# A two-layer GNN block on one core: layer 1's bias and first own part are loaded before layer 0's last transpose, the bounds are computed directly behind their input, and the first z load goes ahead of more of the count loads

## The reference

```python
# block 1: two GraphSAGE layers (mean over the edges, rows = src, cols = dst)
vals  = 1 / deg[rows]                                    # deg: edges per row, 0 -> 1
layer = lambda x, W, b: relu(concat([x, segment_sum(vals * x[cols], rows)]) @ W.T + b)
x = layernorm(x + layer(layer(x, W0, b0), W1, b1))
# block 2: the 32 largest of each row are sent along the edges
h_self, h_neigh = x @ W_self, x @ W_neigh
neigh = segment_sum(top32(h_neigh)[src], dst) / max(deg_dst, 1)
out = layernorm(x + h_self + neigh)
```

## Time and profile before

| | us |
|---|---|
| median of 3 runs | 649.02 (648.73 to 651.68) |
| the profiled execution's own time | 648.15 |
| its span | 646.4 |
| PE busy | 624.2 (97%) |
| DVE, ACT, POOL busy | 487.8, 314.6, 111.9 |
| DMA | 79.62 MB, mean 123 GB/s |
| mean granted TensorE clock | 0.989 |

### The profile page before, as it was taken

One profiled execution on the slowest core, in us unless ns is written; L12 is line 12 of the kernel. 1 busy time (PEld: TensorE's weight loads), 2 busy tenths in 40 slices (PEclk: granted clock), 3 DMA queues, 4 the chain that ended last, 5 costly groups with the idle time before them and its releaser, 6 DMA issues.

```text
span 646.4 us, 10800 instructions
## 1 busy us (share of the span) xinstructions
PE 624.2 (97%) x3750; PEld 322.9 (50%) x3751; DVE 487.8 (75%) x1273; ACT 314.6 (49%) x607; POOL 111.9 (17%) x188
## 2 busy tenths in 40 slices
PE   8689999999999999999998999999999999999996
PEld 4466677776444444444443444444444444444442
DVE  7988999998689998888835688888888910548533
ACT  5769999999397777766721222222232200001000
POOL 2232132222201110110102232232332200000000
PEclk9899999999999999999999999999999999999998
DMA  8535656655422332322214656556564399833200
GB/s 224 135 122 156 217 177 194 192 175 175 125 45 57 71 68 54 68 55 51 71 47 118 147 131 138 131 126 152 133 138 118 83 243 215 211 113 118 86 25 25
DMA packets 66742, 79.62 MB, mean 123 GB/s; under 512 B 30320, under 2 KB 59407, under 8 KB 66681
## 3 DMA queue, kind: packets, MB, share of 16 engines
q1 hardware_dynamic: 66681, 78.86, 47.0%
HBM read 38.91 MB, written 33.38 MB: 112 GB/s over the span
## 4 chain that ended last, share of the span: by engine, by line
PE 65%; ACT 14%; DVE 9%; DMA 7%; issue 3%; SPq 1%; ACTq 0%; POOL 0%; DVEq 0%; POOLq 0%
PE pair L1606 36%; PE bank L1702 8%; ACT slab L1128 7%; PE pair L1702 7%; PE bank L1507 5%; PE pair L1507 4%; DMA a<-z_dram 4%; PE bank L1533 2%; ACT ct L1167 2%; ACT a L1288 2%; DVE hots L673 2%; PE bank L1499 2%; ACT own L1185 1%; PE pair L1419 1%; DMA own_in<-own_dram 1%
## 5 line engine op out<-in xcount | busy, mean ns | idle before, releaser
L1606 PE MATMUL pair<-a,ct 125*128 125x512 f16 x625 | 140.0, 381 | 0.0
L1606 PE MATMUL pair<-xs,ct 125*128 125x512 f16 x625 | 139.1, 379 | 0.0
L1606 PEld LDWEIGHTS pair<-a,ct 125*128 125x128 f16 x625 | 62.5, 100 | 74.9 <-issue 2.1
L673 DVE TENSOR_TENSOR hots<-iota,jobs 125x1792 f16<-125x1792 f16 (+1 forms) x100 | 99.1, 1027 | 0.7 <-ACT jobs L1110 0.7
L1606 PEld LDWEIGHTS pair<-xs,ct 125*128 125x128 f16 x625 | 61.9, 99 | 72.6
L1128 ACT ACTIVATE slab<-pair 125x875 f16<-125x875 f32 (+1 forms) x100 | 83.4, 862 | 4.1 <-DVE matched L720 1.7
L1288 ACT ACTIVATE a<-ct 125x1000 f16<-125x1000 f16 (+1 forms) x75 | 80.4, 1072 | 1.6
L1702 PE MATMUL bank<-xs,ct 125*128 125x512 f16 (+1 forms) x325 | 71.6, 379 | 0.8 <-DVE a L1055 0.8
L563 POOL TENSOR_TENSOR own_in<-own_in,bias_sb 125x256 f32<-125x256 f32 x50 | 37.6, 752 | 171.2 <-DMA own_in<-own_dram 171.1
L1702 PE MATMUL pair<-xs,ct 125*128 125x512 f16 x300 | 66.2, 379 | 0.0
L1355 ACT ACTIVATE sd<-mv,epsb 125x1 f32<-125x1 f32 x25 | 7.3, 294 | 114.8 <-DVE mv L1058 114.8
(11 more groups left out here) (204 smaller groups left out, 776.4 us busy)
## 6 DMA issues: line engine op xcount, KB each, us to landing
c_dram<-slab SPq DMA_DIRECT2D x25, 683.6 KB
ct<-c_dram SPq DMA_DIRECT2D x25, 683.6 KB
own_in<-own_dram SPq DMA_DIRECT2D x50, 125.0 KB
own_dram<-own SPq DMA_DIRECT2D x25, 125.0 KB
own_dram<-own_st SPq DMA_DIRECT2D x25, 125.0 KB
x_in<-in_x_dram SPq DMA_DIRECT2D x25, 125.0 KB
z_dram<-z_st SPq DMA_DIRECT2D x25, 125.0 KB
a<-z_dram SPq DMA_DIRECT2D x5, 625.0 KB
```

Of the source, the lines that this page charges most:

```text
L673: v.tensor_tensor(hots[k][:, :, :, :].rearrange("p w g (a d) -> p (w g) a d", d=2), iota, job, ALU.is_equal).then_inc(win_hot, 1)
L1606: ins = mm(agg[k % 3][0:lhs.shape[1], :], lhs, parts[l][:, t, :], start=t == 0, stop=t == NT - 1, skip_group_check=True)
```

## The change

In SP's program, layer 1's bias and its own block 0 are loaded in the last turn of layer 0's loop, ahead of `turn(24)`; own block 1 goes between the two x loads. The first z load is issued after count loads 12 to 14 instead of 12 to 17. DVE's `bounds()` follows `bound_rows()` at once, where a transpose copy and two one-hot tiles stood between them. POOL's first scaling of `own` waits for all four products of the scales, and not for the scales alone.

```diff
@@ SP, layer 0's loop
             for T in range(NT):
                 if T + 2 < NT:
                     load_own(0, T + 2)
+                if T == NT - 1:
+                    sp.wait_ge(own_biased, NT)
+                    load_bias(1, b1)
+                    load_own(1, 0)
                 turn(T)
                 if T:
                     store_own1(T - 1)
@@ SP, between the layers
             load_x(0)
+            load_own(1, 1)
             load_x(1)
-            sp.wait_ge(own_biased, NT)
-            load_bias(1, b1)
-            load_own(1, 0)
-            load_own(1, 1)
             store_own1(NT - 1)
@@ SP, before the last sum
-            for T in range(NT // 2, 18):
+            for T in range(NT // 2, 15):
                 load_c(T)
@@
             load_z(0)
-            for T in range(18, NT - 1):
+            for T in range(15, NT - 1):
                 load_c(T)
@@ POOL, split_a0
                 if t == 0:
                     pool.wait_ge(scale_ready, 1)
+                    pool.wait_ge(unscale_ready, 4)
@@ DVE, t == 1
                     if t == 1:
                         bound_rows()
+                        bounds()
                         dve.wait_ge(general_ready, 5)
@@
-                    if t == 1:
-                        bounds()
```

## The result

| | us |
|---|---|
| before, median of 5 | 649.15 (648.73 to 651.68) |
| changed, median of 5 | 643.96 (642.81 to 645.71) |
| ratio, with its 95% interval | 0.9922 (0.9895 to 0.995) |
| changed, profiled execution: time, span | 644.75, 643.0 |

The change is 5.1 us faster (3.2 to 6.8); 5.7 us were forecast, as a median of 643.3.

A forecast was written before the change was run, and what follows sets the result against it. The prediction took PE, busy in 97% of the span, as the bound. Its three parts, 3.9 + 1.0 + 0.8 = 5.7 us, taken from 649.02 gave a median of 643.3 us, with a range from 642.1 to 647.0.

The forecast's parts named there:

- The front view: Whole kernel: PE is busy in 97% of the span, so only its idle time and low clock can be won.
- The four waits of the earlier trace: PE's waits for turned parts (2.0 us), bounds (1.1), scales (0.7) and DVE in the last sum (0.8).
- Part A: Layer border: loading bias and own block 0 earlier removes PE's wait and the low clock, 2.05 + 1.84 = 3.9 us.
- the loss of 1.84 us: Layer border: matmuls behind PE's wait run slow at low clock; without idle time ahead, this goes.
- Part B: Front stage: DVE's bounds directly behind their input bring the scales earlier and shorten PE's waits, 1.0 us.
- everything DVE does behind them comes 1.03 us earlier: Front stage: the bounds fill 1.03 us of DVE's idle time, so the scales come at 41.9, not 42.92.
- part B is absorbed: Rival, from 43 us to the layers: something late by its own clock takes 1.0 us back, 644.3; chance 0.15.
- Its own suspect, the stores of the slabs: Within the absorbed rival: slab stores to DRAM that free ACT's buffers may be late by their own clock.
- Part C: Last sum: the first z load behind three count loads fewer lands about 10 us earlier, removing PE's 0.8 us wait.
- the slower rival: Last sum: the second z load comes late, PE idles 4.9 us and loses clock, 650.0; chance 0.04.
- PE waits for DVE near T = 13: Last sum: a sign named beforehand that would show the prediction wrong, at the bank needing the second z load.
- The transpose's being late: Rival at the layer border: block 25's transpose takes a little over 2 us longer, 646.2; chance 0.13.

The follow-up runs named there:

- e9: The changed kernel unaltered, run again on another chip: 643.55 us, ratio 0.9894 to the kernel before.
- e5: The kernel before with 9 idle matmuls where PE waits for the turned parts of block 25: ratio 0.9975, 1.6 us less.
- e2: The kernel before with only the first z load moved ahead of three count loads: ratio 0.9998.
- e3: The kernel before with only the bounds directly behind their input, and POOL's wait for all four products: ratio 0.9993.
- e7: The kernel before with the bounds moved but without POOL's wait for the four products; one execution, no time or ratio given.
- e1: The kernel before with only layer 1's bias and own block 0 loaded ahead of layer 0's last turn: ratio 0.9954, 3.0 us less.
- e4: The change without the moved bounds, so only the early layer 1 loads and early first z load: ratio 0.995, 3.2 us less.
- e6: The change with layer 1's own block 0 loaded directly behind the last turn, not ahead of it: ratio 0.9914.
- e10: The change with the second z load also moved ahead, behind count load 17: 642.68 us, ratio 0.9885.
- e8: The change with 11 idle matmuls in the front stage while PE waits for one-hot tiles: ratio 0.9887.
- e11: The change with front-stage idle matmuls, five more before the last slab's transposes, and the second z load early: 642.43 us, ratio 0.9883.

## Why the prediction was right, point by point

**The front view, right.** PE is the bound, and only its waits could be won. The four waits of the earlier trace rows did what was said in the first profile of the change: three are gone, the fourth shrank. In its second one, e9, the fourth grew to 0.9 us, because PE's first product was fast there and PE came to the scales early.

**Part A, right in mechanism, a little too high.** The landing, the bias add, DVE's start behind the aggregate at 341.9 (343.56 in a profile that is 1.45 us later as a whole, so 342.1), 4.42 us to the issue, no wait: each step is in the trace. Measured alone it gave 3.0 us and not 3.9. The term that was too sure is the clock. The text said that the loss of 1.84 us has no other cause than the idle time, which e5 confirms, and took it as certain to occur, which is wrong: of the four profiles in which PE waits 2.0 to 2.4 us at the border with nothing in between (before, e2, e3, e7), the clock fell in three. Three quarters of 1.84 us and the wait are 3.4 us, inside e1's interval. The one execution of before that I had was one of the three.

**Part B, the step on DVE right, what reaches PE's later path too high.** DVE's part is as forecast: the scales came 11.10 us behind the start of the reduction before, and 10.08 in e3 and e9, the whole 1.02 us. But the step "everything DVE does behind them comes 1.03 us earlier" needs PE to keep up. From the reduction's start to PE's scaled product it was 11.3 us in four of the five profiles without part B (before, e2, e4, e5), and 10.65, 10.30, 10.75, 10.98, 10.30 and 10.88 us in six with it (the change, e3, e6, e7, e9, e10): 10.64 on average, 0.66 us less. The fifth without it, e1, had its first product at half clock throughout and 13.2 us; with it in the average the gain is 1.04 us. I had looked at the order of the waits and not at the clock at that place. PE runs at half clock from 29 us until about 35 to 38 us (40 in e1); in four of those five the wait that part B removes had kept the fp32 product out of that stretch, and now its beginning mostly lies in it: 2.65, 2.10, 2.75, 2.99, 1.93 and 2.89 us in these six, instead of 1.98. In e8 and e11, with the clock up, the product takes 1.93 us and the way from the reduction to the scaled product 9.88 us.

Then comes a term that the prediction put at nothing, POOL's new wait. By the estimate under e7, its delay of the store of `own` takes 0.5 to 0.6 us back at 53 us in five of the seven profiles with it. At PE's fp32 product near 65 us (64.84 before, 64.05 in the change) the same six profiles (e7 among them, which lacks that wait) are 0.31 us ahead of the same four, 32.71 against 33.02 us behind the reduction, or 0.70 us with e1 among those without. So "part B is absorbed", given 0.15, came true in part, through the stores of `own` as far as the traces tell. Its own suspect, the stores of the slabs, adds losses too: they move with ACT, as the prediction said, but they land within the loop's 4.93 us by nothing, so some come late in kernels with and without part B. The copies of `ct` that were to stay covered made PE wait 0.60 us in e9 and 1.21 in e8 and e11; PE then waits for the scales all the same, so this costs nothing.

**Part C, right in mechanism, too low as an average.** The first z came 8.4 us (e2) and 9.2 us (the change) earlier relative to PE, for the 9.6 forecast. The 0.8 us of the one profile is the smallest of five: 0.78, 1.04, 1.35, 1.77 and 2.06 us where six count loads stand ahead of z (before, e1, e3, e5, e7), none in the eight profiles where three do. On average 1.4 us (the clock fell behind one of them, e7's, and cost 1.7 us more). Against it stands the second z load, which I had as the slower rival with 1.5 us of room before and 0.7 after. The room is 1.5 to 2.5 us in four profiles without part C, and 0.3 to 1.3 us in four of the six with only the first z early (the change, e4, e8, e9); in the other two, e2 and e6, there is none and PE waited 0.65 and 0.46 us. "PE waits for DVE near T = 13" was a sign of being wrong, so on this point the prediction was wrong in two of six. That z(0) holds up the loads behind it fits this; its size is far from the 3.9 us of idle time that would have turned the sign. e10 removes it. Its time alone (e2) shows nothing, so C's worth rests on the traces.

**The sum, near by luck in part.** With these averages from the traces A comes to 3.4 and not 3.9, B to 0.3 or 0.7 (with e1) and not 1.0, C to 1.2 (1.4 less 0.2 for the second z) and not 0.8: 4.9 to 5.3 us. A and B were set too high, C too low, and the errors cancel in part. 5.1 us were measured at first and 6.9 later, 5.7 forecast.

**The other points.** POOL's wait wins nothing on the path, and by the estimate under e7 it costs 0.5 to 0.6 us in five of seven profiles. The transpose's being late, given 0.13, did not occur in any of the eight profiles with part A. That own block 0 had to go ahead of the transpose was not needed (e6); the loads that stood ahead of it were what had to be passed.

What stays open: what the change is worth without POOL's wait, why the store of `own` takes 6.2 to 6.4 us in five profiles and less than 5.9 us in two, why the slab stores land late at this slab and not at that, and why the clock falls behind one wait of 2 us and not behind another. No run here varied any of these by itself. The parts' own times below about 1.5 us couldn't be told from no change.

## What to carry to other kernels

A wait of an engine that is the bound costs its length and, on PE, perhaps a few us at half clock behind it; read the matmuls' durations behind each wait, and count that loss as a chance, from more than one execution. When a wait is removed, look at the clock of the stretch that the work now moves into: it may have been shielding that work from a slow one. And a load that is late is often only behind other small loads; moving it past those is enough. Last, a wait added to an engine off the path is not free: ask which store or load is issued behind that engine's work, in order, and who waits for its buffer.

## What the runs showed of the hardware that was not expected

- Idle time of PE at the border of 2.05, 2.00 and 2.33 us (before, e2, e3) brought its clock from 2.4 to 1.2 GHz, and 2.38 us (e7) did not; 2.06 us did so in the last sum (e7), and 1.77 us there did not (e5, where the 25 matmuls behind it took 5.56 us). Near 161 us, 1.53 us (the change) and 1.40 us (e3) were followed by a fall (granted clock 0.76 and 0.72 from 160 to 166 us), and 1.44 us (e1) and 1.39 us (e2) were not. So the length of the wait alone does not decide. Filling the time with matmuls whose result nobody reads kept the clock up each time it was tried (e5, e8, e11).
- Loads of 125 partitions by 1 KB landed one behind the other, each some 1.1 us after the one ahead (own blocks 0 and 1 of before were biased at 344.07 and 345.12, in e6 with an x load between them at 339.31 and 341.53). A load that takes 4.2 us behind two transfers takes 7.9 behind five.
- A store of 125 partitions by 1 KB took 6.2 to 6.4 us from issue to landing in five profiles, behind two slab stores, and less than 5.9 us in two others (at 45 to 52 us).
- A loop of 4.93 us whose store to DRAM takes 4.8 to 5.0 us to land lost 0.3 to 0.96 us at up to three slabs of 25, at different ones in different executions.
